# Self-attention: the transposes of one head of each pair go from TensorE to VectorE and SyncE's DMAs, and the products one double unit later

## What is computed

```python
q = jnp.einsum('bne,ef->bnf', x, wq).reshape(B, N, HEADS, DHEAD).transpose(0, 2, 1, 3)
...
scores = jnp.einsum('bhnd,bhmd->bhnm', q, k) * SCALE
attn = jax.nn.softmax(scores, axis=-1)
out = jnp.einsum('bhnm,bhmd->bhnd', attn, v)
out = out.transpose(0, 2, 1, 3).reshape(B, N, HEADS * DHEAD)
return jnp.einsum('bnf,fe->bne', out, wo) + bo
```

## Time and profile before

| | us |
|---|---|
| Time, median of 3 runs (lowest, highest) | 1038.58 (1038.11, 1039.63) |
| Span of the profiled execution | 1036.7 |
| Self-attention, first project_v of the steady order to last x update | 175.0 to 790.0 |
| TensorE busy | 981.3, 95% |
| VectorE, ScalarE, GpSimd busy | 690.3, 591.5, 380.1 |
| Chain of waits, share by engine | TensorE 64%, VectorE 10%, ScalarE 5% |

### The profile page before, as it was taken

The page is one execution under the profiler, slowest core; times in us unless marked ns, Lnnn a source line. Parts: engine busy times, 40 slices in busy tenths (PEclk is TensorE's granted clock), DMA queues, the critical chain, the costliest instruction groups (busy, mean ns, idle before and its releaser), DMA issues.

```text
span 1036.7 us, 17534 instructions
## 1 busy us (share of the span) xinstructions
PE 981.3 (95%) x6376; PEld 707.1 (68%) x6376; DVE 690.3 (67%) x1171; ACT 591.5 (57%) x1332; POOL 380.1 (37%) x493
## 2 busy tenths in 40 slices
PE   7999978999999999999999999999989999999998
PEld 4566666666667656667666667666647589999887
DVE  2767646677773776773676773776753889999563
ACT  2666634766763667763667763667753555455442
POOL 2576623434332344342344341343330024444220
PEclk9999999999999999999999999999999999999999
DMA  6400050000000000000000000000000340000000
GB/s 134 94 2 1 1 147 1 1 1 2 1 1 2 1 1 2 1 1 1 2 1 1 1 1 1 2 1 1 2 1 8 101 110 1 1 1 1 2 26 26
DMA packets 25370, 17.64 MB, mean 17 GB/s; under 512 B 8565, under 2 KB 24101, under 8 KB 25285
## 3 DMA queue, kind: packets, MB, share of 16 engines
q1 hardware_dynamic: 25285, 16.52, 6.6%
HBM read 11.26 MB, written 1.31 MB: 12 GB/s over the span
## 4 chain that ended last, share of the span: by engine, by line
PE 64%; DVE 10%; ACT 5%; issue 4%; POOL 1%; DMA 0%; SPq 0%; DVEq 0%; ACTq 0%; POOLq 0%
PE banks L409 13%; PE banks L396 12%; PE banks L382 11%; PE banks L416 4%; ACT sa_probs L499 3%; PE banks L224 3%; PE banks L227 2%; PE banks L226 2%; PE banks L225 2%; PE banks L1641 2%; PE banks L1933 2%; DVE sa_negmax L571 2%; DVE ca_top L1776 2%; DVE ca_probs L1781 1%; PE banks L232 1%
## 5 line engine op out<-in xcount | busy, mean ns | idle before, releaser
L639 POOL TENSOR_SCALAR sa_probs<-sa_probs,sa_inverse 128x512 f32<-128x512 f32 x320 | 217.7, 696 | 372.4 <-DVE sa_inverse L575 372.3
L499 ACT ACTIVATE sa_probs<-banks,sa_negmax 128x512 f32<-128x512 f32 x320 | 215.8, 685 | 163.5 <-DVE sa_negmax L571 163.4
L571 DVE TENSOR_REDUCE sa_negmax<-banks 128x2 f32<-128x1024 f32 x160 | 188.8, 1219 | 12.4 <-PE banks L382 9.7
L396 PEld LDWEIGHTS banks<-ident,sa_probs 128*128 128x128 f32 x1280 | 145.7, 141 | 55.6 <-issue 27.6
L396 PE MATMUL banks<-ident,sa_probs 128*128 128x128 f32 x1280 | 174.0, 277 | 10.0 <-ACT sa_turned L510 5.8
L580 DVE COPY sa_turned<-banks 128x512 f32<-128x512 f32 x160 | 110.2, 689 | 76.3 <-PE banks L396 76.3
L409 PE MATMUL banks<-sa_turned,sa_v 128*64 128x512 f32 x640 | 155.0, 605 | 0.0
L382 PE MATMUL banks<-sa_k_parts,sa_q_parts 64*128 64x512 f32 x960 | 134.9, 412 | 1.9 <-ACT sa_probs L499 1.9
L510 ACT COPY sa_turned<-banks 128x512 f32<-128x512 f32 x160 | 94.3, 590 | 30.6 <-PE banks L396 28.8
L382 PEld LDWEIGHTS banks<-sa_k_parts,sa_q_parts 64*128 64x128 f32 x960 | 85.2, 187 | 31.2 <-issue 14.4
L409 PEld LDWEIGHTS banks<-sa_turned,sa_v 128*64 128x64 f32 x640 | 38.7, 136 | 74.3 <-issue 73.0
(11 more groups left out here) (218 smaller groups left out, 1724.9 us busy)
## 6 DMA issues: line engine op xcount, KB each, us to landing
w_o<-in_L_xattn_wo SPq DMA_DIRECT2D x2, 800.0 KB, 9.2
out<-x SPq DMA_DIRECT2D x4, 320.0 KB, 2.4
w_q_t<-in_L_xattn_wq_t SPq DMA_DIRECT2D x1, 1120.0 KB, 10.4
fold_values<-ca_turned SPq DMA_DIRECT2D x5, 192.5 KB
x<-in_x SPq DMA_DIRECT2D x1, 960.0 KB, 5.8
fold_values<-ca_probs SPq DMA_DIRECT2D x4, 192.5 KB
w_q_t<-in_L_xattn_wq SPq DMA_DIRECT2D x1, 640.0 KB, 6.6
w_o<-in_L_xattn_wk SPq DMA_DIRECT2D x1, 640.0 KB, 10.0
```

What stands on the lines that cost most here:

```text
L396: last = pe.transpose(b_turn[e][:, q * P:(q + 1) * P], probs[:, j % 2, e, q, k * P:(k + 1) * P], ident[:])
L499: act.activation(probs[:, j % 2, e, q, :], b_scores[u % 2][:, e, :], ACT.Exp, bias=negmax[:, u % RING, e:e + 1], accum_out=total[:, u % RI ...
L571: dve.tensor_reduce(negmax[:, u % RING, :], b_scores[u % 2], AX_X, ALU.max, negate=True).then_inc(s_max.sem, 1)
L639: pool.tensor_scalar(probs[:, j % 2, e, q, :], probs[:, j % 2, e, q, :], inverse[:, u % RING, e:e + 1], 1.0, ALU.mult, ALU.mult).then_inc( ...
```

## The change

The two heads of a pair part ways. The second head's probabilities (`probs_turn`) are transposed by TensorE as before, now alone, into one bank `b_turn`, and ScalarE copies them. The first head's (`probs_flip`) are transposed by VectorE in 32x32 blocks (`flip`, four a pair, each 128x512) into `flipped`. A block transpose leaves every block in its own group of 32 partitions, so SyncE moves the blocks between the groups: when the fourth `flip` of a pair is done it issues 16 DMAs (4 source groups x 4 destination groups, each 32 partitions with one run of 2 KB) into `placed`, 640 in all. The first product of the pair waits for all 16 (`wait_placed`). In `placed` the query order is by block, so ScalarE's copies bring the second head into the same order (`by_group`, `by_block`) and `att` back out of it. `pv` runs two double units behind (PV_LAG = 2), not one, and crosses from one batch into the next; the output projection is spread over the double units 1 to 3 of the next batch and has the bank `b_x`; `update` follows in 3 and 4. The tile `raw_tail` of the adapter is released before the self-attention, and the area for GpSimd's DMA descriptors is set to 4096.

```diff
@@ selfattn: constants and tiles
-    V_BUF = (0, 1, 2, 0, 1)
-    V_BEFORE = (3 - 5, 4 - 5, 2 - 5, 0, 1)
+    V_BUFS = 3
     RING = 8
+    GROUP = 32
+    GROUPS = P // GROUP
+    FLIP_RING, TURN_RING = QT, QT
+    PV_LAG = 2
...
-        probs = sb("probs", [P, 2, 2, QT, S])
-        turned = sb("turned", [P, 2, 2, S])
+        probs_flip = sb("probs_flip", [P, FLIP_RING, S])
+        probs_turn = sb("probs_turn", [P, 2, QT, S])
+        flipped = sb("flipped", [P, 2, GROUPS, QT, QT, GROUP])
+        placed = sb("placed", [P, 2, GROUPS, QT, QT * GROUP])
+        turned = sb("turned", [P, TURN_RING, S])
...
-        b_scores, b_turn, b_out, b_proj = [banks.pair(0), banks.pair(2)], banks[4:6], banks[6], banks[7]
+        b_scores, b_x, b_turn, b_out, b_proj = [banks.pair(0), banks.pair(2)], banks[4], banks[5], banks[6], banks[7]
...
+        def wait_placed(eng, b, j):
+
+            m = b * NPAIR + j
+            if m >= 0:
+                eng.wait_ge(s_placed[m % 2], 16 * GROUPS * GROUPS * (m // 2 + 1))
...
+        by_group = lambda ap: ap.rearrange("p (i n c) -> p n i c", i=GROUPS, n=QT)
+        by_block = lambda ap: ap.rearrange("p (n i c) -> p n i c", i=GROUPS, n=QT)
+
+        @block.sync
+        def _(sp):
+            for b in range(B):
+                for j in range(NPAIR):
+                    m = b * NPAIR + j
+                    sp.wait_ge(s_flip.sem, s_flip.at(b, QT * j + QT - 1))
+                    sp.wait_ge(s_pv.sem, s_pv.at(b, QT * (j - 1) - 1))
+                    for i in range(GROUPS):
+                        for g in range(GROUPS):
+                            sp.dma_start(placed[g * GROUP:(g + 1) * GROUP, m % 2, i, :, :],
+                                         flipped[i * GROUP:(i + 1) * GROUP, m % 2, g, :, :, :].rearrange("p k n c -> p k (n c)")).then_inc(s_placed[m % 2], 16)
@@ TensorE
                 j, k = divmod(u, QT)
                 if k == 0:
                     pe.wait_ge(s_norm.sem, s_norm.at(b, 2 * QT * j + 2 * QT - 1))
-                for e in range(2):
...
-                    for q in range(QT):
-                        last = pe.transpose(b_turn[e][:, q * P:(q + 1) * P], probs[:, j % 2, e, q, k * P:(k + 1) * P], ident[:])
-                    last.then_inc(s_turn.sem, 1)
+                pe.wait_ge(s_evac.sem, s_evac.at(b, u - 1))
+                for q in range(QT):
+                    last = pe.transpose(b_turn[:, q * P:(q + 1) * P], probs_turn[:, j % 2, q, k * P:(k + 1) * P], ident[:])
+                last.then_inc(s_turn.sem, 1)
 
             def pv(b, u):
...
+                pe.wait_ge(s_evac.sem, s_evac.at(b, u))
                 if k == 0:
                     pe.wait_ge(s_vsb.sem, s_vsb.at(b, j | 1))
                     pe.wait_ge(s_att.sem, s_att.at(b, j - 1))
+                    wait_placed(pe, b, j)
+                moving = (placed[:, (b * NPAIR + j) % 2, :, k, :], turned[:, u % TURN_RING, :])
...
             def batch(b, more):
                 for d in range(ND):
                     norm, _, nb = following(b, more)
-                    if d >= 1:
-                        pv(b, 2 * d - 2)
-                        pv(b, 2 * d - 1)
+                    for u in (2 * (d - PV_LAG), 2 * (d - PV_LAG) + 1):
+                        if u >= 0:
+                            pv(b, u)
+                        elif b > 0:
+                            pv(b - 1, u + NU)
+                    if b > 0 and d == 2:
+                        project_out(b - 1, 1)
                     if d % 2 == 0:
                         over(next_v, b, d // 2 + 2, NPAIR, more)
...
                     turns(b, 2 * d + 1)
+                    if b > 0 and d in (2, 3):
+                        project_out(b - 1, d)
                     for i in range(2):
                         over(scores, b, 2 * (d + LEAD + 1) + i, NU, more)
-
-                pv(b, NU - 2)
-                pv(b, NU - 1)
-                project_out(0, 0, NPAIR - 1)
-                pe.wait_ge(s_att.sem, s_att.at(b, NPAIR - 1))
-                project_out(0, NPAIR - 1, NPAIR)
-                for q in range(1, QT):
-                    last = project_out(q, 0, NPAIR)
-                    if q % 2 == 1:
-                        last.then_inc(s_o.sem, 1)
+                    if b > 0 and d == 1:
+                        project_out(b - 1, 0)
 
             over_batches(pe, batch)
+            for u in range(NU - 2 * PV_LAG, NU):
+                pv(B - 1, u)
+            for q in range(QT):
+                project_out(B - 1, q)
@@ ScalarE
             def exps(b, u):
                 j, q = divmod(u, QT)
                 act.wait_ge(s_max.sem, s_max.at(b, u))
+                act.wait_ge(s_flip.sem, s_flip.at(b, u - FLIP_RING))
...
-                act.copy(att[:, j, :], b_out).then_inc(s_att.sem, 1)
+                act.copy(by_block(att[:, j, :]), by_group(b_out)).then_inc(s_att.sem, 1)
...
-                act.copy(turned[:, u % 2, 1, :], b_turn[1]).then_inc(s_evac_act.sem, 1)
+                act.wait_ge(s_turn.sem, s_turn.at(b, u))
+                act.wait_ge(s_pv.sem, s_pv.at(b, u - TURN_RING))
+                act.copy(by_group(turned[:, u % TURN_RING, :]), by_block(b_turn)).then_inc(s_evac.sem, 1)
@@ VectorE
-                dve.tensor_copy(turned[:, u % 2, 0, :], b_turn[0]).then_inc(s_evac.sem, 1)
...
+            def flip(b, u):
+                j, n = divmod(u, QT)
+                dve.wait_ge(s_norm.sem, s_norm.at(b, 2 * u))
+                if n == 0:
+                    wait_placed(dve, b, j - 2)
+                dve.transpose(flipped[:, (b * NPAIR + j) % 2, :, :, n, :].rearrange("p g k c -> p k g c"),
+                              probs_flip[:, u % FLIP_RING, :].rearrange("p (k g c) -> p k g c", k=QT, g=GROUPS)).then_inc(s_flip.sem, 1)
...
                     if d % 2 == 0:
                         over(copy_v, b, d // 2 + 2, NPAIR, more)
-                    copy_turned(b, 2 * d)
+                    over(flip, b, m - 2, NU, more)
                     over(inverses, b, m + 1, NU, more)
-                    copy_turned(b, 2 * d + 1)
+                    over(flip, b, m - 1, NU, more)
+                    if b > 0 and d in (3, 4):
+                        update(b - 1, d - 3)
```

More of the change, by code:

```diff
@@ L321, in selfattn @@
         s_noted = ctx.enter_context(nc.semaphore("sa_inverse_noted"))
-        s_turn = sig("turned_made", 2 * NU, 4 * QT)
-        s_evac = sig("turned_copied", NU, 2)
-        s_evac_act = sig("turned_copied_act", NU, 2)
+        s_flip = sig("flipped_made", NU, FLIP_RING)
+        s_placed = [ctx.enter_context(nc.semaphore(f"sa_placed{i}")) for i in range(2)]
+        s_turn = sig("turned_made", NU, 2 * QT)
+        s_evac = sig("turned_copied", NU, TURN_RING)
         s_pv = sig("pv_made", NU, 6 * QT)
@@ L406, in pv, with project_out @@
                     pe.wait_ge(s_att.sem, s_att.at(b, j - 1))
+                    wait_placed(pe, b, j)
+                moving = (placed[:, (b * NPAIR + j) % 2, :, k, :], turned[:, u % TURN_RING, :])
                 for e in range(2):
                     c = j % 2 * P + e * HD
-                    last = pe.matmul(b_out[e * HD:(e + 1) * HD, :], v[:, V_BUF[j // 2], k, c:c + HD],
-                                     turned[:, u % 2, e, :], start=(k == 0), stop=(k == QT - 1))
+                    last = pe.matmul(b_out[e * HD:(e + 1) * HD, :], v[:, v_buffer(b, j), k, c:c + HD],
+                                     moving[e], start=(k == 0), stop=(k == QT - 1))
                 last.then_inc(s_pv.sem, 1)
[L413 to L418, removed]
+            def project_out(b, q):
+                if q == 0:
+                    pe.wait_ge(s_att.sem, s_att.at(b, NPAIR - 1))
+                    pe.wait_ge(s_x.sem, s_x.at(b, -1))
+                if q == QT - 1 and b < B - 1:
+                    pe.wait_ge(s_x.sem, s_x.at(b, 0))
+                for j in range(NPAIR):
+                    last = pe.matmul(x_place(b, q), att[:, j, q * P:(q + 1) * P], w_o[:, j, :], start=(j == 0), stop=(j == NPAIR - 1))
+                if q >= QT - 2:
+                    last.then_inc(s_o.sem, 1)
             ln.ready(pe, 0)
@@ L540, in batch @@
                     copy_turned(b, 2 * d + 1)
-                copy_att(b, NPAIR - 1)
+                    if d % 2 == 1 and d > PV_LAG:
+                        copy_att(b, (d - PV_LAG) // 2)
+                    if d == 1 and b > 0:
+                        copy_att(b - 1, NPAIR - 1)
             over_batches(act, batch)
+            copy_att(B - 1, NPAIR - 1)
         @block.vector
         def _(dve):
-            for s in (s_qlo, s_klo, s_vsb, s_evac, s_x):
+            for s in (s_qlo, s_klo, s_vsb, s_flip, s_x):
                 dve.sem_inc(s.sem, s.credit)
@@ L627, in batch @@
                         norm.standardize(dve, nb)
-                update(b)
             over_batches(dve, batch)
+            for part in range(2):
+                update(B - 1, part)
         @block.gpsimd
@@ L2063, in build @@
```

(6 more changed lines are left out.)

79 lines of the change are left out of this document (37 added, 42 removed).

## The result

The changed kernel takes 1165.02 us (median of 4 runs, 1161.61 to 1169.42) against 1038.34 us (1037.45 to 1039.63) for the kernel before on the same chip: a ratio of 1.122, with a 95% interval of 1.119 to 1.124. The prediction had 1155 us.

A forecast was written before the change was run, and what follows sets the result against it. TensorE bounds the kernel before; in the change, a loop of 5.2 + 9.9 + 2.1 = 17.2 us, plus 0.9 for the clock, gives 18.1 us a pair, 116 us more in all: 1155 us, 8-in-10 range 1080 to 1290.

The forecast's parts named there:

- the loop: From one pair's first product through project_v, copy of v, block transposes, 16 issues and landing to the next: 17.2 us.
- first product to SyncE's first issue: Products and project_v 3.1 us, then copy of v, block transposes, reciprocal and SyncE's seeing it: 5.2 us a pair.
- fifteen issues: SyncE's 15 further DMA issues after a pair's first, at 0.66 us each: 9.9 us.
- landing and start: Landing of a pair's last regrouping DMA, with the start of the product: 2.1 us.
- clock: Waiting in every pair lowers TensorE's clock for the products and projection after it: 0.9 us a pair, between nothing and 3.1.
- last two pairs: At the end of the self-attention, no projection ahead of their block transposes, bound by issues alone: 21.1 us.
- rival with 0.88: SyncE's issues as dear as the cross-attention's, 0.88 us each: 22.0 us a pair, 1310 us in all; chance 13%.
- the one with 0.47: SyncE's issues as cheap as the plain load, 0.47 us each: 14.3 us a pair, 1004 us in all; chance 8%.
- three quarters of it fall into TensorE's waits: Of each batch's output projection, only the quarter ahead of project_v at d=2 lies on the loop: 3 x 2.7 = 8.1 us.
- 4 to 6 us, 40 times: Sign in the profile: TensorE's longest wait, at L440 for the DMA sa_placed, once in each pair.
- the rival in which everything is hidden: Issue cost does not hold back the data; TensorE runs at 12.4 us a pair, 972 us in all; chance 3%.
- the prediction's 4.4 us: A pair's megabyte of regrouping transfers by the Trainium skill's rule, an estimate below the 7.2 us that there are.

The follow-up runs named there:

- e7: Changed kernel with products three double units behind instead of two, and b_x as second turning bank for odd units: 1004.0 us, ratio 0.967.
- e9: Changed kernel, otherwise as it is, with b_x as second turning bank for odd units: 1177.4 us, ratio 1.134.
- e10: Changed kernel with GpSimd issuing source groups 2 and 3, and b_x as second turning bank for odd units: 1011.8 us, ratio 0.974.
- the swap: Both block transposes put ahead of VectorE's copy of v in even double units: 1063.9 us on the changed kernel, 1032.8 us on e7.
- e6: Changed kernel with source groups 2 and 3 issued by GpSimd, 0 and 1 by SyncE: 1028.0 us, ratio 0.989.

## Why the prediction was right

The mechanism held: undoing any one link of the loop (lag, issues in a row, order of VectorE) takes back 100 to 137 us, and halving the bytes 13.5. The prediction's steps one by one (three of the 37 pairs, one at each batch boundary, hold three quarters of an output projection; the means are over the other 34):

| Step | Predicted | Measured |
|---|---|---|
| first product to SyncE's first issue | 5.2 | 5.1 at full clock |
| fifteen issues | 15 x 0.66 = 9.9 | 9.7 in the mean, 0.645 each; 9.6 from 458.9 to 468.6 |
| landing and start | 2.1 | 2.1 to 2.2 |
| loop at full clock | 17.2 | 16.65 the shortest, 16.9 with the mean of the issues |
| clock | 0.9 | 1.1 |
| block transpose of 128x512 | 0.68 | 0.69 |
| pair, mean of the 34 | 18.1 | 18.05 |
| the three pairs at batch boundaries | 18.1 + 2.7 = 20.8 | 21.84 |
| mean of the 37 pairs | 18.1 + 8.1 / 37 = 18.3 | 18.36 |
| first product of pair 0 | at 191.2 | at 191.1 |
| last two pairs | 21.1 | 870.41 to 897.43: 27.0 |
| tail | 15.8 | 897.43 to 913.3: 15.8 |
| floor of a pair off the loop | 12.4 | 12.44 the shortest in mid-course, 13.2 the median (e7) |
| end of the self-attention | 906 | 913.3 |

The rows for the issues and for the two ends:

```profile
L370 SPq DMA_DIRECT2D sa_placed<-sa_flipped x16: 507/590/592, 458.9 to 468.6; - x16
```

```profile
870.41 0.61 PE L440 MATMUL banks<-sa_placed,sa_v 128*64 128x512 f32 x1 [0.99 <-DMA sa_placed<-sa_flipped]
...
872.34 0.69 DVE L623 STREAM_TRANSPOSE sa_flipped<-sa_probs_flip 128x512 f32<-128x512 f32 x1
...
884.58 1.08 PE L440 MATMUL banks<-sa_placed,sa_v 128*64 128x512 f32 x1 [4.15 <-DMA sa_placed<-sa_flipped]
...
897.43 0.61 PE L440 MATMUL banks<-sa_placed,sa_v 128*64 128x512 f32 x1 [1.36 <-ACT sa_att L544]
...
912.93 0.32 DVE L635 TENSOR_TENSOR x<-banks,x 128x160 f32<-128x160 f32 x1 [2.06 <-PE banks L452]
```

**Issues.** "I take 0.66, near the middle and near the 0.65 row" was right to 0.015 us, 9 us over all issues. The rival with 0.88 was wrong, and the one with 0.47 too: an issue from SBUF to SBUF took longer than the plain load of 32 rows from HBM into SBUF. Whether that is the source or something else of the two was not tried.

**The clock** came out at 6.24 - 5.12 = 1.1 us a pair, against 0.9. The loop without it was 0.3 us shorter than the sum, so the pitch of 18.05 agrees with 18.1 by two errors that cancel; that the agreement is so close is luck. The prediction took the clock as a constant, and it varies: 16 of the 36 waited starts are at half clock, after waits of 2.2 to 4.5 us, and the other 20, after waits of 0.5 to 3.6 us, are not, so the length of the wait alone does not tell which. That also answers "the granted clock is below 1 through the whole self-attention": on average (0.92), but single pairs are at 1.00.

**The output projection** costs more than "three quarters of it fall into TensorE's waits" allows. Three of its quarters lie in one pair, and with them TensorE's own work exceeds the loop. That pair runs at full clock and ends without a wait:

```profile
375.99:397.84 21.85, 20.75 (x132) 15.38 (x133) 8.30 (x14) 6.59 (x15) 4.05 (x6) 1.00 0.20 49
```

```profile
397.84 0.64 PE L440 MATMUL banks<-sa_placed,sa_v 128*64 128x512 f32 x1
```

It takes 3.8 us more than a mean pair, where 2.7 were predicted, three times: 3 us in all. The same pairs take 21.8 us in all runs with a lag of two and 21 with a lag of three, so no cure of the loop reaches them.

**The last two pairs** are 6 of the 7 us by which the end of the self-attention was missed. They are not "bound by issues alone". For the first, SyncE's issues begin only 2.65 us after the product of the pair before, behind a block transpose that ends at 873.03, and the landing stands on the path too: 2.65 + 9.4 + 2.1 = 14.2 us in place of 10.6. The second's product did not wait for a transfer at all, but for a copy out of `b_out` by ScalarE, after products that started at half clock (884.58): 12.8 us. Another 3 us lie outside the sum: the profiled execution took 1161.6 us, 1.8 over its span as assumed, and is the lowest of the four.

**"4 to 6 us, 40 times"** was read too simply off 17.2 - 12.4. The waits at L440 are 0.5 to 4.5 us, 95.7 us in 36 times; the rest of a pair's slack is in half-clock work and in the waits for the one turning bank, 37.3 us at L426. That bank was in no step of the prediction: with the loop it costs nothing (e9), without it 16 to 26 us (e10, e7), and so the experiments on this side came out above their expectations. The 972 us of the rival in which everything is hidden was not reached. In e7 the updates (L647) of the first three batches start at 343.96, 487.57 and 629.61, so a batch takes 142.8 us: 10 x 12.44 + 11.1 for the output projection + 7.3. The kernel before has more of such a loss than the 4.7 us that the rival dropped, for its 153.5 us a batch average in the shorter last one. There the updates of the first three batches are 156.65 us apart (VectorE's timeline), 137.7 + 11.1 + 7.9:

```profile
323.37 0.49 DVE L588 TENSOR_TENSOR x<-banks,x 128x320 f32<-128x320 f32 x1 [8.24 <-PE banks L416]
...
480.02 0.49 DVE L588 TENSOR_TENSOR x<-banks,x 128x320 f32<-128x320 f32 x1 [8.24 <-PE banks L416]
```

So 7.3 of 7.9 us stayed with the output projection spread. The spreading by itself was not tried.

The Trainium skill (DMA: Bandwidth & Descriptors, section Anatomy of one DMA) gives the fit behind the prediction's 4.4 us for transfers that GpSimd issues. The prediction used it for SyncE's.

## What to carry to other kernels

When a step moves from a compute engine to transfers, find the loop that it closes: count the issues of one queue in a row, multiply by the pitch of the nearest issue row, add the landing and the engine work on both sides, and compare with the bottleneck's time per turn. If it is longer, one more stage of lag, or a second issuer, is worth far more than fewer bytes (here 135 and 137 us against 13.5). Then look for the next limit, here the one turning bank and the output projection, and look again after each cure, since the swap that gained 101 us in the loop lost 29 us outside it.

## What had not been expected of the hardware

- An issue's length did not depend on its bytes: 591 ns in the median for 64 KB and for 32 KB. GpSimd's issues of the same transfers took 498 ns. With both engines issuing (e6), the median landing was 2.3 us for GpSimd's and 2.5 for SyncE's, against 2.0 with SyncE alone.
- Relieving TensorE in a kernel bound by another loop made it slower by 12 us, with a granted clock of 0.90 against 0.92 and a front of the loop longer by 0.4 us a pair.
- A block transpose of 128x512 float32 in VectorE, with its regrouping pattern, takes 0.69 us, as long as a plain copy of that size from PSUM.
